# A graph network kernel: the scale of x is found inside the counting loop, x's last part is loaded behind the store of the edge rows, and the second half of a search is placed at the 52nd window

## What is computed

```python
# x: (6250, 128) f32; src, dst: (106250,), sorted by dst; edge_attr_64: (106250, 64)
agg = segment_sum(x[src], dst, num_segments=6250)          # the sum over edges
h   = relu((x + agg) @ W1.T + b1); h = relu(h @ W2.T + b2)  # layer 0
x   = layernorm(x + h)
x   = layernorm(x + gcn(x, ...))      # layer 1: four such sums, with degree factors
x   = layernorm(x + edge_gcn(x, ...)) # layer 2: also sums edge_attr_64 @ We over edges
x   = layernorm(x + sage(x, ...))     # layer 3: two such sums
```

## Time and profile before

| | us |
|---|---|
| Median of 3 runs | 2571.49 |
| Lowest and highest | 2568.89, 2573.13 |
| The profiled execution | 2577.17 |
| Its span, from the first instruction to the last | 2575.4 |
| PE busy | 2471.7 (96%) |
| DVE busy | 1310.4 (51%) |
| ACT busy | 599.5 (23%) |

### The profile page before, as it was taken

The page is one execution under the profiler, slowest core; times in us unless marked ns, Lnnn a source line. Parts: engine busy times, 40 slices in busy tenths (PEclk is TensorE's granted clock), DMA queues, the critical chain, the costliest instruction groups (busy, mean ns, idle before and its releaser), DMA issues.

```text
span 2575.4 us, 38445 instructions
## 1 busy us (share of the span) xinstructions
PE 2471.7 (96%) x15593; PEld 1451.4 (56%) x15593; DVE 1310.4 (51%) x3605; ACT 599.5 (23%) x717; POOL 162.6 (6%) x117
## 2 busy tenths in 40 slices
PE   2889999899999999999999999999999999999998
PEld 1778899645555555555555555554445555555545
DVE  7887788467877666676656333332222122122222
ACT  3878999560000111111111000000000000000000
POOL 4000000010000111111111000000000200000000
PEclk9999999999999999999999999999999999999999
DMA  5736222346776666666666565545554554545553
GB/s 163 90 100 78 99 99 99 152 116 215 242 232 206 186 197 182 188 177 189 184 190 179 147 190 140 140 137 141 143 142 124 154 140 134 141 137 148 158 152 110
DMA packets 294910, 395.37 MB, mean 154 GB/s; under 512 B 82248, under 2 KB 282564, under 8 KB 291268
## 3 DMA queue, kind: packets, MB, share of 16 engines
q1 hardware_dynamic: 243960, 326.08, 45.7%
q10 hardware_dynamic: 49964, 64.80, 7.8%
q0 software_dynamic: 800, 1.94, 0.3%
HBM read 343.43 MB, written 49.32 MB: 153 GB/s over the span
## 4 chain that ended last, share of the span: by engine, by line
PE 89%; DVE 3%; DMA 2%; issue 2%; SPq 1%; ACT 1%; DVEq 1%; POOL 1%; ACTq 0%; POOLq 0%
PE PS L1709 83%; PE PS L1893 1%; SPq L530 1%; PE PS L1900 1%; PE PS L1901 1%; DVE TB L962 1%; PE PS L1915 1%; DMA edge_rows<-AT 1%; POOL AT L671 0%; PE PS L1845 0%; PE PS L1924 0%; PE PS L1895 0%; PE PS L1954 0%; DMA HR<-adjacency 0%; PE PS L1873 0%
## 5 line engine op out<-in xcount | busy, mean ns | idle before, releaser
L1709 PE MATMUL PS<-HR,HN 128*128 128x500 fp8e3 (+1 forms) x5096 | 1061.3, 365 | 1.9 <-DVE HN L1129 1.5
L1709 PE MATMUL PS<-HR,AGN 128*128 128x500 fp8e3 (+1 forms) x4606 | 917.9, 350 | 4.0 <-DMA HR<-adjacency 2.2
L1709 PEld LDWEIGHTS PS<-HR,HN 128*128 128x128 f16 x5096 | 489.0, 97 | 521.0 <-issue 9.5
L1709 PEld LDWEIGHTS PS<-HR,AGN 128*128 128x128 f16 x4606 | 446.6, 97 | 401.0 <-issue 3.0
L1709 PE MATMUL PS<-TB 128*128 128x245 f16 x1250 | 321.9, 277 | 28.5 <-DVE TB L962 20.3
L962 DVE TENSOR_TENSOR TB<-HN,HR 128x1240 f16<-128x1240 f16 x250 | 199.6, 798 | 0.0
L1206 DVE SCALAR_TENSOR_TENSOR AT<-PS,SC,TB 128x384 f32<-128x384 f32 (+24 forms) x50 | 21.6, 472 | 324.1 <-PE PS L1709 315.4
L1709 PEld LDWEIGHTS PS<-TB 128*128 128x128 f16 x1250 | 123.6, 100 | 54.3 <-DVE TB L962 13.2
L962 DVE TENSOR_TENSOR TB<-iot,HN 128x640 f16<-128x640 f16 x250 | 122.2, 489 | 62.6 <-PE PS L1709 61.9
L751 POOL TENSOR_TENSOR AT<-AT,dstI 128x1088 f32<-128x1088 f32 x49 | 100.2, 2045 | 740.8 <-DVE mxe L1332 740.8
L1359 DVE TENSOR_SCALAR TB<-iot,dstF 128x118 f16<-128x118 f16 (+1 forms) x833 | 142.0, 252 | 6.2 <-PE PS L1709 0.4
(11 more groups left out here) (248 smaller groups left out, 1672.9 us busy)
## 6 DMA issues: line engine op xcount, KB each, us to landing
HR<-adjacency SPq DMA_DIRECT2D x588, 437.5 KB, 3.5
AT<-source_lanes ACTq DMA_DIRECT2D x49, 544.0 KB, 4.9
AT<-in_edge_attr_dram ACTq DMA_DIRECT2D x144, 128.0 KB, 3.0
adjacency<-HN SPq DMA_DIRECT2D x9, 1531.2 KB, 5.7
adjacency<-HR SPq DMA_DIRECT2D x8, 1531.2 KB, 5.8
adjacency<-TB SPq DMA_DIRECT2D x8, 1531.2 KB, 5.5
HR<-adjacency SPq DMA_DIRECT2D x49, 218.8 KB, 2.5
AT<-in_edge_attr_dram ACTq DMA_DIRECT2D x48, 160.0 KB, 4.1
```

The source lines that it names most:

```text
L1709: return t_.matmul(out_, w, m, start=start, stop=True, skip_group_check=True)
```

## The change

Five things are different, and no arithmetic is.

1. SP waits for the eight stores of the edge rows (`s_rows`) before it issues the third part of x. All that stands behind it in SP's queue stays behind it.
2. The first two parts of x (five sevenths) are measured where they were. The third part, the largest value of all, and the scale are now made in the loop ahead of window 15 (`MEASURE_AT`), in another PSUM bank (`MSX`). So `decode` of the first two groups no longer has them ahead of it. PE's two small matmuls move with them, behind its first 15 windows.
3. ACT spreads the first slots at once and makes the seven high parts inside stage 0, one each ahead of its copies 4 to 10. Each still waits for the scale.
4. DVE's seven low parts stand at windows 26, 30, ... 50, where they stood at 12, 16, ... 36.
5. `find_edge(WA, WG)` stands at window 52 instead of 20, and the decoding behind it at 112, 118, ... 154 instead of 90, 96, ... 132.

```diff
--- before.py
+++ after.py
@@ -294,6 +294,8 @@
         Y, Z, Y2, X2, X1 = (PS[:, 512 * k:512 * k + MOST] for k in (3, 4, 5, 6, 7))
         AG1 = PS[:, 3584:3584 + 2 * SD_]
         MS = PS[:, 2048:2048 + P + 1]
+
+        MSX = PS[:, 3584:3584 + P + 1]
         N1, N2 = PS[:, 512:512 + 4 * P], PS[:, 2048:2048 + 3 * P + 3]
         PB, PC = PS[:, 3072:3072 + P], PS[:, 3584:3584 + P]
 
@@ -451,6 +453,8 @@
             return len(range(m, PCS, RING))
 
 
+        MEASURE_AT = 15
+
         TURN_AT = {170: 2, 184: 4, 220: 6, 234: 8}
         WEIGHT_AT = {270: (0, 4), 286: (4, 6)}
         assert WA == 2 and WG == 10
@@ -504,6 +508,9 @@
                 sp.dma_start(dstK[p0:p1, :], a["dst"][p0 * KJ:p1 * KJ].rearrange("(p j) -> p j", j=KJ)).then_inc(s_keys, 16)
             sp.dma_start(dstK[127:128, 0:KL], a["dst"][127 * KJ:E].rearrange("(o j) -> o j", o=1)).then_inc(s_keys, 16)
             for k, (q0, q1) in enumerate(XPARTS):
+                if k == 2:
+
+                    sp.wait_ge(s_rows, 16 * SH)
                 b0, b1 = QB * q0, min(QB * q1, NB - 1)
                 sp.dma_start(blk(XN)[:, b0:b1, :], rows(a["x"][b0 * P:b1 * P, :])).then_inc(s_x[k], 16)
             sp.dma_start(blk(XN)[0:NTAIL, NB - 1, :], a["x"][(NB - 1) * P:N, :]).then_inc(s_x[2], 16)
@@ -780,7 +787,7 @@
 
             def measure_line(n):
                 dve.wait_ge(s_c2, n)
-                v.tensor_reduce(m1[:, :], MS[0:1, 0:P], axis=AX, op=ALU.max).then_inc(s_c3, 1)
+                v.tensor_reduce(m1[:, :], (MSX if n == 1 else MS)[0:1, 0:P], axis=AX, op=ALU.max).then_inc(s_c3, 1)
 
             def low_x(q):
                 cols = slice(q * QN, (q + 1) * QN)
@@ -927,12 +934,6 @@
             measure_x(0)
             find_edge(0, WA)
             measure_x(1)
-            measure_x(2)
-            measure_lane(NQ)
-            measure_line(1)
-            dve.wait_ge(s_c4, 1)
-            scale_of(0, MS[:, P:P + 1])
-            dve.drain().then_inc(s_scale, 1)
             for step in range(8):
                 decode(step, 0, WA)
             dve.wait_ge(s_ltp, 1)
@@ -989,12 +990,19 @@
                     last_windows(t // SUBW - 1)
                 if t % SUBW == 20 and t > SUBW:
                     diagonal(t // SUBW - 1)
-                if t == 20:
+                if t == MEASURE_AT:
+                    measure_x(2)
+                    measure_lane(NQ)
+                    measure_line(1)
+                    dve.wait_ge(s_c4, 1)
+                    scale_of(0, MSX[:, P:P + 1])
+                    dve.drain().then_inc(s_scale, 1)
+                if t == 52:
                     find_edge(WA, WG)
-                if t in range(12, 12 + 4 * NQ, 4):
-                    low_x((t - 12) // 4)
-                if t in range(90, 90 + 6 * 8, 6):
-                    decode((t - 90) // 6, WA, WG)
+                if t in range(26, 26 + 4 * NQ, 4):
+                    low_x((t - 26) // 4)
+                if t in range(112, 112 + 6 * 8, 6):
+                    decode((t - 112) // 6, WA, WG)
                 if t in range(200, 200 + 6 * 8, 6):
                     count((t - 200) // 6)
                 if t in range(260, 260 + 6 * 3, 6):
@@ -1451,13 +1459,14 @@
             for k in range(SH):
                 o_ = k * (KROWS * P - STEP)
                 act.dma_start(flat_rows[o_:o_ + P * KJ].rearrange("(p j) -> p j", j=KJ), KP).then_inc(s_rows, 16)
-            act.wait_ge(s_scale, 1)
-            for q in range(NQ):
-                if q == 3:
-                    act.wait_ge(s_ltp, 1)
-                    c.copy(V4[0][:, 0:WA * P, :], PS[:, 0:WA * P].unsqueeze(2).to_broadcast([P, WA * P, REP])).then_inc(s_ct, 1)
+            act.wait_ge(s_ltp, 1)
+            c.copy(V4[0][:, 0:WA * P, :], PS[:, 0:WA * P].unsqueeze(2).to_broadcast([P, WA * P, REP])).then_inc(s_ct, 1)
+
+            def high_x(q):
                 cols = slice(q * QN, (q + 1) * QN)
+                act.wait_ge(s_scale, 1)
                 c.activation(HI[0][:, cols], XN[:, cols], ACT.Copy, scale=SC[:, 0, 0:1]).then_inc(s_hi, 1)
+
             def sub_sums(s):
                 act.wait_ge(s_un, s + 1)
                 c.activation(AT[:, SD_ * s:SD_ * (s + 1)], AG2[s % 2], ACT.Copy, scale=SC[:, 0, 1:2]).then_inc(s_at, 1)
@@ -1468,6 +1477,8 @@
                     act.wait_ge(s_un, s - 2)
                 a3 = A16[s % 3].rearrange("p (h w d) -> p w h d", h=NB, d=WD)
                 for k, (i0, i1) in enumerate(EV[:NEA]):
+                    if s == 0 and 4 <= k < 4 + NQ:
+                        high_x(k - 4)
                     if k == 1 and s == 7:
                         act.wait_ge(s_lot, 1)
                         c.copy(LOB[:, 0:(LKC - 1) * P], LTP[:, 0:(LKC - 1) * P])
@@ -1713,17 +1724,15 @@
 
             def measured_lane(n):
                 pe.wait_ge(s_c1, n)
-                t_.matmul(MS[0:1, 0:P], mx[:, 0:1], ident[:, :], start=True, stop=True).then_inc(s_c2, 1)
+                t_.matmul((MSX if n == 1 else MS)[0:1, 0:P], mx[:, 0:1], ident[:, :], start=True, stop=True).then_inc(s_c2, 1)
 
             def measured_line(n):
                 pe.wait_ge(s_c3, n)
-                t_.matmul(MS[:, P:P + 1], ones[0:1, :], m1[0:1, 0:1], start=True, stop=True).then_inc(s_c4, 1)
+                t_.matmul((MSX if n == 1 else MS)[:, P:P + 1], ones[0:1, :], m1[0:1, 0:1], start=True, stop=True).then_inc(s_c4, 1)
 
             pe.wait_ge(s_cst, 1)
             pe.wait_ge(s_smf, 1)
             t_.matmul(SMP, ones[0:1, :], smpF, start=True, stop=True).then_inc(s_smb, 1)
-            measured_lane(1)
-            measured_line(1)
             pe.wait_ge(s_dec, 1)
             for k, t in enumerate((LF, CF)):
                 for g in range(WA):
@@ -1749,6 +1758,9 @@
                 done = 0
                 for i in range(SUBW):
                     t = SUBW * s + i
+                    if t == MEASURE_AT:
+                        measured_lane(1)
+                        measured_line(1)
                     if t == 6 * SUBW:
                         pe.wait_ge(s_wtc, 6)
                         pe.wait_ge(s_at, 4)
```

## The result

The changed kernel takes 2585.28 us in the median of 6 runs (2582.18 to 2587.96), the kernel before 2570.64 on the same chip (6 runs, 2568.04 to 2573.45). The ratio is 1.0054, with a 95% interval of 1.0044 to 1.0064, which is 11.3 to 16.5 us; the medians differ by **14.6 us**. The forecast was 2587.3, so 15.8. The profiled execution took 2583.96.

A forecast was written before the change was run, and what follows sets the result against it. The first 108 us were taken as bound by search, gathers, index loads and store of stage 0, PE having no slack from 188 us; the store's 15.8 us delay made 2575.4 into 2591.2, on the median 2587.3, range 2582 to 2593.

The forecast's parts named there:

- The bound: First 108 us: one chain of search, eight gathers, index loads and store of stage 0; DVE, ACT, PE wait at stage 3.
- The loop's start: Ahead of the loop: edge-row stores land 1.5 us earlier, decoding starts at 32.4, loop at 38.2 instead of 39.78.
- a gather takes 4.16 to land ... and 0.3 for x beside it: Second gather behind the edge-row stores, ahead of decoding: 4.16 us from issue to landing, 0.3 more for x.
- The scale, the high and low parts: Stage 0: scale takes 4.81 us, DVE goes on at 46.4, seventh high part 15.9 later, search ends at 68.7.
- The gathers: POOL behind the search: 1.68 us each, 11.7 from first to last; last issued at 80.8, landed at 84.95.
- Index loads and store: SP's queue behind the gathers: 31.1 us to the store of stage 0, 6.26 for the store, landed at 122.3.
- What arrives: From stage 3 on: ACT comes at about 105.4 and waits 17 us; all 15.8 us of the store's delay reach the end.
- its sign: ACT's wait for the store of stage 0, at stage 3, would be 15 to 20 us instead of 6.
- The sign that failed: From the first store's landing to the end: a distance changed by more than 2 us would prove the forecast wrong.
- the wait does not matter: Rival at stage 3: no pause for PE, 4.9 us paid in stage 0, 6.0 saved, about 2570.4 us; chance 0.05.
- The stores were bunched: Rival in SP's queue: store of stage 0 takes 10.6 us among others, 4.3 more lost, 2591.6 us; chance 0.08.
- the early start of the loop: Rival: a later pause hides that at stage 3, only the loop's 1.6 us gain arrives, 2569.9 us; chance 0.05.

The follow-up runs named there:

- a_search20: Changed kernel with the second half of the search back at window 20, decoding left at 112 to 154; 2576.22 us, ratio 1.0023 to the kernel before.
- b_search52: Kernel before with only the search moved to window 52 and its decoding to 112 to 154; 2577.78 us, ratio 1.0027 to the kernel before.
- a_noxwait: Changed kernel without SP's wait ahead of x's third part; 2583.74 us, ratio 1.0049 to the kernel before.
- b_lowlate: Kernel before with DVE's seven low parts moved from windows 12 to 36 to windows 46 to 52; 2570.34 us, ratio 0.9995 to the kernel before.
- b_xwait: Kernel before with only x's third part held back behind the stores of the edge rows; 2575.36 us, ratio 1.0014 to the kernel before.
- b_again: Unchanged copy of the kernel before, run for a second profile; 2571.39 us, ratio 0.9999 to the kernel before.
- a_again: Unchanged copy of the changed kernel, run for a second profile; 2585.63 us, ratio 1.0054 to the kernel before.
- a_idx: Changed kernel with SP's index loads and their wait for the gathers put behind the store of stage 0; 2576.02 us, ratio 1.0019 to the kernel before.
- b_idx: Kernel before with SP's index loads and their wait for the gathers put behind the store of stage 0; 2565.76 us, ratio 0.9982 to the kernel before.

## Why the prediction was right, point by point

**The bound.** Right: the store of stage 0 still ends the chain, ACT and PE stand still until it has landed, and the delay at the landing (12.6) is the delay at the mark (12.5). a_search20 and b_search52 show that the search's place moves it.

**The loop's start.** 38.76 measured, 38.2 forecast. The reason was half wrong. The stores landed 1.7 earlier, as forecast (1.5), but the step "a gather takes 4.16 to land ... and 0.3 for x beside it" was mis-sized, since it took 5.2 for the two. The wait for the stores, which I priced as a gain, is worth nothing (a_noxwait), and the start is earlier for the second reason alone, the scale out of the way.

**The scale, the high and low parts.** The one-hot groups took 3.36, the scale 4.78 (42.12 to 46.90), so E, the time at which DVE goes on behind the scale, is 46.90 for 46.4. The seventh high part was done at 62.5, E + 15.6 (forecast 15.9), and the search at 69.13, E + 22.2 (22.3; 68.7). These steps held within 0.3. DVE's rows:

```profile
42.12 2.07 DVE L932 TENSOR_REDUCE MX<-XN 128x1 f32<-128x896 f32 x2
...
46.90 0.49 DVE L963 TENSOR_TENSOR TB<-iot,HN 128x640 f16<-128x640 f16 x1 [0.17 <-issue]
...
61.44 2.40 DVE L795 SCALAR_TENSOR_TENSOR AGN<-XN,SC,AGN 128x896 f16<-128x896 f32 x2
```

**The gathers.** Here the size was off. They went at 1.39 us each, not at 1.68: 9.8 us instead of 11.7. The rows at 61.62 and 64.97 from which I took the 1.68 stood where DVE was busy all the time (7.00 of 7 us, from 62 to 69), while behind the late search DVE waits for PE. The 2.00 that I gave for low parts was a mean over seven gathers, two of them beside one-hot matrices; the five beside low parts took 2.13 each. The Trainium skill (SBUF — State Buffer, "Who interferes with whom") says that a `tensor_tensor` was not seen to stall a DMA issued from GpSimd. By the rows here that is nearly so: 1.39 is near the idle pace of 1.25, but the 1.61 in b_lowlate, beside one-hot matrices without a gap, is not. The landing took 2.90 instead of 4.16, a price that I had taken unquestioned from the one row. The last gather's landing spreads widely, from 2.58 in b_xwait to 4.68 in a_search20, and nothing here says why.

**Index loads and store.** 82.17 to 113.61 is 31.4 (31.1 forecast). The store took 5.5 instead of 6.3. From the terms: +0.4 for the search's end, -1.9 for the gathers' pace, -1.3 for the last landing, +0.3 for the loads, -0.7 for the store give the 3.2 by which the landing (119.1) came earlier than forecast (122.3).

**What arrives.** ACT came to stage 3 at 106.6 (105.4) and so waited 12.5, not the forecast 17, and outside of the 15 to 20 that I had named as its sign. PE was not idle from 109 to 123 either, as I had said: it was busy from 110 to 114, at a granted clock of 0.57 in the mean, and stood still only from 114.3 to 120.4. The median moved by 14.6, 2.1 more than the mark. That is no finding: the interval goes down to 11.3. But the forecast is nearer to the median than its own sum is to the trace: the sum gave 15.8 us, the trace shows 12.5 and the median 14.6. That nearness is luck.

**The sign that failed.** I wrote that a distance from the landing to the end changed by more than 2 us would speak against the forecast. It changed by 5.8 between the first profiles, and by 0.5 between the second profiles (b_again and a_again). A single profile can't carry a test of 2 us over 2460 us; the marks up to 200 us agree within 0.4.

**The rival "the wait does not matter".** It did not come, and its price was wrong too. I had 4.9 lost and 6.0 won for it, 2570.4. a_idx makes just that case, with the store landed in time, and takes 2576.0. The 6.0 are there (6.2 from before to b_idx), but the change costs 11.2 on its own (b_idx to a_idx) and not 4.9, and each of its three blocks (scale, late search, late decoding) shows at the mark. DVE's slack of only 6.3 us up to the store of stage 4 (b_idx) is the likely reason. "What is late next" was the question that I answered for ACT alone. With the gate in place these 11 us run beside the gate's delay and add nothing to it: from the landing to the mark it is 81.6 us in after and 81.7 in before. This is why the forecast did not suffer from it.

**The other rivals.** Neither came. The stores were bunched, three of them issued from 113.61 to 114.61, but the first took 5.5 us and not 10.6. And the early start of the loop did not decide, since the mark moved with the landing of the store.

## What to carry to other kernels

When a queue in program order holds a store behind loads that nobody needs yet, move the loads behind the store before tuning anything that feeds them: here that edit alone gave 4.6 us, while moving work around it lost 14.6. Before an edit at the head of a chain is priced, ask which engine is next if the chain were free, and how much slack it has; two causes of about the same size can hide each other, and undoing one of them gives back only part. A transfer that is held back to free the queues for one step can land on the next step: look at what runs beside it then.

## What the runs showed of the hardware that I had not expected

- An indirect gather on POOL took 0.94 us with little beside it, 1.82 to 1.88 next to low parts (`scalar_tensor_tensor`, f32 and f16 in, f16 out, 896 wide, 1.1 us each). Some that began beside a low part and went on beside one-hot matrices took 2.94 and 4.05; why is not shown.
- A gather's time from issue to landing was 2.6 us in a_noxwait and 5.2 in after, with 331 GB/s of loads beside it. But load is not all: the last gather took 4.16 in before and 4.57 in b_lowlate with only 35 and 32 GB/s moved.
- In after PE stood idle from 66.3 to 71.0. The granted clock is 1.00 (2.4 GHz) in the stretches around it, yet the windows' matmuls took 0.41 us until 76 and 0.27 from then on. In a_again the granted clock reads 0.50 from 56 to 74 us, and the same matmuls took the same 0.41, until 74.8. The two marks lie 0.4 us apart. So the matmuls' own durations have to be read beside the granted clock. In PE's timeline of after:

```profile
71.40 0.41 PE L1720 MATMUL PS<-TB 128*128 128x245 f16 x1
...
76.30 0.27 PE L1720 MATMUL PS<-TB 128*128 128x245 f16 x1
```

- Behind the long pause at stage 3 PE's clock was granted at 0.50 up to 124 us and at 1.00 from then on:

```profile
119.00:124.00 5.00, 3.59 (x18) 2.63 (x19) 1.21 (x2) 4.76 (x5) 0.00 (x0) 0.50 1.02 429
124.00:130.00 6.00, 6.00 (x58) 5.57 (x57) 3.62 (x6) 5.32 (x6) 0.00 (x0) 1.00 0.24 102
```
